# Grouped attention: three rounded products for scores and values, probabilities scaled on GpSimd, a weight split in four pieces

## The reference, cut to what matters

```python
B, SQ, HIDDEN = (2, 256, 256)
HEADS, GROUPS, KVC = (16, 4, 128)
HPG = HEADS // GROUPS
LAYER_INDEX = 1
SCALE = KVC ** (-0.5)
b, sq, _ = x.shape
...
q = jnp.einsum('bsh,he->bse', x, w_q).reshape(b, sq, GROUPS, HPG, KVC)
kv = jnp.einsum('bsh,he->bse', x, w_kv)
k, v = jnp.split(kv, 2, axis=-1)
...
scores = jnp.einsum('bqgpd,bkgd->bgqpk', q, k) * (SCALE / LAYER_INDEX)
...
causal = jnp.arange(sq)[:, None] >= jnp.arange(sk)[None, :]
scores = jnp.where(causal[None, None, :, None, :], scores, -jnp.inf)
probs = jax.nn.softmax(scores, axis=-1).astype(x.dtype)
ctx = jnp.einsum('bgqpk,bkgd->bqgpd', probs, v).reshape(b, sq, HEADS * KVC)
return jnp.einsum('bse,eh->bsh', ctx, w_dense)
```

## Time and profile before

| | |
|---|---|
| median of 3 runs (lowest to highest) | 1756.77 us (1753.88 to 1758.28) |
| profiled execution, its time | 1758.49 us |
| profiled execution, first to last instruction (span) | 1756.7 us |
| mean granted clock of TensorE | 0.955 |
| busy over the span: TensorE, VectorE, ScalarE, GpSimd | 1578.6, 1052.2, 868.1, 376.4 us |
| grouped attention (258.2 to 535.7 us): TensorE, VectorE, ScalarE, GpSimd busy | 260.78, 143.35, 136.96, 16.48 us |

### The profile page before, as it was taken

How to read it: one execution, slowest core, us unless ns; L and a number is a source line. 1 busy time by engine, 2 the same in 40 slices (tenths; PEclk the granted TensorE clock), 3 DMA queues, 4 the chain that set the end, 5 groups by cost and what they waited for, 6 DMA issues and landing times. The chain is left out here.

```text
span 1756.7 us, 27299 instructions
## 1 busy us (share of the span) xinstructions
PE 1578.6 (90%) x9658; PEld 1270.8 (72%) x9658; DVE 1052.2 (60%) x2079; ACT 868.1 (49%) x1931; POOL 376.4 (21%) x400
## 2 busy tenths in 40 slices
PE   7789989999999889998678869879999999997987
PEld 6568866766768768886356646658888888875966
DVE  2665445374465544445558750657878787876965
ACT  2443334454455333333357643446666666664634
POOL 0044531011002054543454212101101010001300
PEclk9789989999999899999889988899999999998999
DMA  4131111000000463220144320100000000001000
GB/s 119 48 116 49 48 33 35 6 13 18 0 0 1 128 156 99 77 79 1 26 69 62 39 74 1 44 21 16 19 9 18 9 18 18 9 1 50 1 0 25
DMA packets 76099, 68.23 MB, mean 39 GB/s; under 512 B 32176, under 2 KB 67208, under 8 KB 76016
## 3 DMA queue, kind: packets, MB, share of 16 engines
q1 hardware_dynamic: 71312, 62.73, 13.5%
q0 software_dynamic: 4704, 4.40, 2.0%
HBM read 56.46 MB, written 1.21 MB: 33 GB/s over the span
## 5 line engine op out<-in xcount | busy, mean ns | idle before, releaser
L2326 ACT ACTIVATE diff_att_probs<-psum,diff_att_neg_max 128x512 f32<-128x512 f32 x256 | 174.4, 695 | 27.3 <-DVE diff_att_neg_max L2388 27.3
L2388 DVE TENSOR_REDUCE diff_att_neg_max<-psum 128x2 f32<-128x1024 f32 x128 | 153.1, 1218 | 24.1 <-PE psum L2226 24.1
L2247 PE MATMUL psum<-diff_att_v_tok,diff_att_mixed_t 128*128 128x128 f32 x1024 | 127.5, 279 | 0.8 <-ACT diff_att_mixed_t L2332 0.8
L2247 PEld LDWEIGHTS psum<-diff_att_v_tok,diff_att_mixed_t 128*128 128x128 f32 x1024 | 124.3, 196 | 4.5 <-issue 1.8
L1346 ACT ACTIVATE gqa_att_probs<-psum,gqa_att_neg_max 128x128 f32<-128x128 f32 (+3 forms) x128 | 66.4, 524 | 69.0 <-DVE gqa_att_neg_max L1378 69.0
L472 POOL TENSOR_TENSOR ahead_w_hi<-ahead_w,ahead_zeros 128x512 fp32r<-128x512 f32 x16 | 16.6, 1039 | 375.2 <-DMA ahead_w<-in_L_attn_Wv 375.1
L1378 DVE TENSOR_REDUCE gqa_att_neg_max<-psum 128x1 f32<-128x128 f32 (+3 forms) x128 | 53.8, 483 | 70.0 <-PE psum L1296 69.0
L892 POOL TENSOR_TENSOR top_scaled<-top_scaled,top_wb 128x512 f32<-128x512 f32 x48 | 65.3, 1366 | 117.1 <-DVE top_scaled L871 87.1
L2400 DVE SCALAR_TENSOR_TENSOR diff_att_mixed<-diff_att_probs,diff_att_ratio 128x512 f32<-128x512 f32 x128 | 87.7, 748 | 1.1
L871 DVE TENSOR_TENSOR top_scaled<-top_gate,psum 128x512 f32<-128x512 f32 x48 | 32.9, 687 | 86.5 <-PE psum L101 64.6
L1640 POOL DMA_DIRECT2D mla_att_q_own<-mla_att_parts x144 | 71.0, 502 | 54.5 <-PE psum L1726 50.5
(11 more groups left out here) (480 smaller groups left out, 4586.3 us busy)
## 6 DMA issues: line engine op xcount, KB each, us to landing
top_wb<-top_w_dram SPq DMA_DIRECT2D x16, 384.0 KB, 4.1
golden_wb<-golden_w_dram SPq DMA_DIRECT2D x8, 512.0 KB, 4.8
top_wb<-top_w_dram SPq DMA_DIRECT2D x16, 256.0 KB, 4.3
mla_att_k_feat<-mla_att_parts SPq DMA_DIRECT2D x56, 64.0 KB, 4.5
mla_att_q_own<-mla_att_parts POOLq DMA_DIRECT2D x112, 32.0 KB, 3.5
top_w_nat<-in_L_ffn_w SPq DMA_DIRECT2D x16, 192.0 KB, 3.1
top_w_nat<-in_L_ffn_v SPq DMA_DIRECT2D x16, 192.0 KB, 4.2
top_down_w<-in_L_ffn_w SPq DMA_DIRECT2D x1, 3072.0 KB, 13.2
```

The lines of the kernel that those rows point to most:

```text
L2247: last = nc.tensor.matmul(bank[6][:, qt * P:(qt + 1) * P], mixed_t[:, u % 2, kt, qt * P:(qt + 1) * P], v_tok[:, slot, b * QT + kt, :], sta ...
L2326: last = nc.scalar.activation(probs[:, qt, m, :], bank[2 * (qt % 2) + m], ACT.Exp, bias=neg_max[:, qt, m:m + 1], accum_out=row_sum[:, qt, ...
L2388: nc.vector.tensor_reduce(neg_max[:, qt, :], psum[:, 2 * (qt % 2):2 * (qt % 2) + 2, :], AX.X, ALU.max, negate=True).then_inc(maxed, 1)
```

## The change

The scores and the values become three rounded products each. For that every projection is rounded to a high part by ScalarE (now q_hi, k_hi, v_hi) and VectorE subtracts it from the bank to get the low part (`lower_projection`); a bank is free for the next job when the low part is made. The turned probabilities are treated in the same way: ScalarE copies banks 4 and 5 to `pt_hi`, VectorE bank 7, and VectorE makes the three low parts (`lower_turned`). `attend` waits bank by bank. The scaling of the probabilities moves from VectorE to GpSimd, as a multiplication by a reciprocal that is spread over the row. The split of the next group's weights is cut in its four instructions, which stand on GpSimd ahead of the scaling of units 2 to 5. The probabilities are packed without gaps.

```diff
+
+    def split_part(self, pool, g, i):
+
+        nc, t, rounded = self.nc, self.t, self.sem["w_rounded"]
+        n = "kq"[i % 2]
+        raw, high, low = (t[f"w{n}_{part}"] for part in ("g", "hi", "lo"))
+        if i == 0:
+            pool.wait_ge(self.sem["w_loaded"], g * 48 + 48)
+        if i < 2:
+            nc.gpsimd.tensor_tensor(high[:], raw[:], t["zeros"][:].to_broadcast([P, DC, raw.shape[2]]), ALU.add).then_inc(rounded, 1)
+        else:
+            pool.wait_ge(rounded, g * 2 + (i - 1))
+            nc.gpsimd.tensor_tensor(low[:], raw[:], high[:].bitcast(F32), ALU.subtract).then_inc(self.sem["w_split"], 1)
 
...
-            q_feat = at.sb("q_feat", [P, HPG, T])
-            k_feat = at.sb("k_feat", [P, T])
-            v_tok = at.sb("v_tok", [P, NT, HD])
-            probs = at.sb("probs", [P, 2, QT, SEQ])
-            probs_t = at.sb("probs_t", [P, QT, SEQ])
+            q_hi, q_lo = (at.sb(f"q_{n}", [P, HPG, T], F32R) for n in ("hi", "lo"))
+            k_hi, k_lo = (at.sb(f"k_{n}", [P, T], F32R) for n in ("hi", "lo"))
...
+            probs = at.sb("probs", [P, 2, PACKED])
+            pt_hi, pt_lo = (at.sb(f"pt_{n}", [P, PACKED], F32R) for n in ("hi", "lo"))
+            row = lambda s, qt: probs[:, s, qt * (qt + 1) // 2 * P:(qt + 1) * (qt + 2) // 2 * P]
+            turned = [slice(0, 4 * P), slice(4 * P, 7 * P), slice(7 * P, 10 * P)]
+            turned_bank = [bank[4], bank[5][:, 0:3 * P], bank[7][:, 0:3 * P]]
...
-                with pool.Fori(1, GROUPS) as g:
-                    pool.wait_ge(proj_made, g * JOBS)
-                    pre.split(pool, g)
+                def normalise(g, u):
+                    s = u % 2
+                    pool.wait_ge(inverted, g * UNITS + (u + 1))
+                    for qt in range(QT):
+                        tile = row(s, qt)
+                        last = nc.gpsimd.tensor_tensor(tile, tile, inv_sum[:, s, qt:qt + 1].to_broadcast([P, (qt + 1) * P]), ALU.mult)
+                    last.then_inc(probs_ready, 1)
+
+                with pool.Fori(0, GROUPS - 1) as g:
+                    for u in range(UNITS):
+                        if 2 <= u < 6:
+                            pre.split_part(pool, g + 1, u - 2)
+                        normalise(g, u)
+                for u in range(UNITS):
+                    normalise(GROUPS - 1, u)
...
-                        pe.wait_ge(proj_read, g * JOBS + (j - 2))
+                        pe.wait_ge(proj_low, g * JOBS + (j - 2))
...
-                        nc.tensor.matmul(bank[qt][:, 0:(qt + 1) * P], q_feat[:, h, b * SEQ + qt * P:b * SEQ + (qt + 1) * P],
-                                         k_feat[:, b * SEQ:b * SEQ + (qt + 1) * P], start=True, stop=False)
+                        queries = slice(b * SEQ + qt * P, b * SEQ + (qt + 1) * P)
+                        keys = slice(b * SEQ, b * SEQ + (qt + 1) * P)
+                        product3(nc, bank[qt][:, 0:(qt + 1) * P], (q_hi[:, h, queries], q_lo[:, h, queries]),
+                                 (k_hi[:, keys], k_lo[:, keys]), start=True, stop=False)
...
-                    pe.wait_ge(t_read_act, g * UNITS + (u + 1))
-                    pe.wait_ge(t_read_dve, g * (2 * UNITS) + 2 * (u + 1))
                     if u:
                         pe.wait_ge(ctx_read, g * UNITS + u)
+                    at = 0
                     for kt in range(QT):
-                        last = nc.tensor.matmul(bank[6][:, kt * P:SEQ], v_tok[:, b * QT + kt, :],
-                                                probs_t[:, kt, 0:SEQ - kt * P], start=kt == 0, stop=kt == QT - 1)
+                        if kt < 3:
+                            pe.wait_ge(t_low, g * (3 * UNITS) + (3 * u + kt + 1))
+                        part = slice(at, at + SEQ - kt * P)
+                        at += SEQ - kt * P
+                        last = product3(nc, bank[6][:, kt * P:SEQ], (v_hi[:, b * QT + kt, :], v_lo[:, b * QT + kt, :]),
+                                        (pt_hi[:, part], pt_lo[:, part]), start=kt == 0, stop=kt == QT - 1)
...
-                        causal_transposes(nc, env, lambda qt: probs[:, u % 2, qt, :], t_made)
+                        causal_transposes(nc, env, lambda qt: row(u % 2, qt), t_made)
...
+                        read = nc.scalar.activation(q_hi[:, h, cols], job_bank(j), ACT.Copy, scale=SCALE)
                     elif kind == "k":
...
-                        act.wait_ge(t_made, g * (3 * UNITS) + (3 * u + 1))
-                        nc.scalar.activation(probs_t[:, 0, :], bank[4][:], ACT.Copy).then_inc(t_read_act, 1)
+                        for k in range(2):
+                            act.wait_ge(t_made, g * (3 * UNITS) + (3 * u + k + 1))
+                            nc.scalar.activation(pt_hi[:, turned[k]], turned_bank[k], ACT.Copy).then_inc(t_high_act, 1)
...
-                    dve.wait_ge(inverted, g * UNITS + (u + 1))
-                    for qt in range(QT):
-                        tile = probs[:, s, qt, 0:(qt + 1) * P]
-                        last = nc.vector.tensor_scalar(tile, tile, inv_sum[:, s, qt:qt + 1], None, ALU.mult)
-                    last.then_inc(probs_ready, 1)
...
+                def lower_projection(g, j):
+                    kind, h, half = jobs[j]
+                    cols, tiles = slice(half * HALF, (half + 1) * HALF), slice(4 * half, 4 * half + 4)
+                    dve.wait_ge(proj_high, g * JOBS + (j + 1))
+                    if kind == "q":
+                        low = nc.vector.scalar_tensor_tensor(q_lo[:, h, cols], job_bank(j), SCALE, q_hi[:, h, cols].bitcast(F32),
+                                                             ALU.mult, ALU.subtract)
+                    elif kind == "k":
+                        low = nc.vector.tensor_tensor(k_lo[:, cols], job_bank(j), k_hi[:, cols].bitcast(F32), ALU.subtract)
...
+                    low.then_inc(proj_low, 1)
...
+                def lower_turned(g, u, k):
+                    if k < 2:
+                        dve.wait_ge(t_high_act, g * (2 * UNITS) + (2 * u + k + 1))
+                    else:
+                        dve.wait_ge(t_high_dve, g * UNITS + (u + 1))
+                    nc.vector.tensor_tensor(pt_lo[:, turned[k]], turned_bank[k], pt_hi[:, turned[k]].bitcast(F32),
+                                            ALU.subtract).then_inc(t_low, 1)
...
                 with dve.Fori(0, GROUPS) as g:
-                    maxima(g, 0)
-                    normalise(g, 0)
+                    for j in range(JOBS):
+                        lower_projection(g, j)
+                        if j == EARLY:
+                            maxima(g, 0)
+                        if j == JOBS - 2:
+                            normalise(g, 0)
                     for u in range(UNITS):
                         if u + 1 < UNITS:
                             maxima(g, u + 1)
-                        dve.wait_ge(t_made, g * (3 * UNITS) + (3 * u + 2))
-                        nc.vector.tensor_copy(probs_t[:, 1, 0:3 * P], bank[5][:, 0:3 * P]).then_inc(t_read_dve, 1)
+                        lower_turned(g, u, 0)
                         dve.wait_ge(t_made, g * (3 * UNITS) + (3 * u + 3))
-                        nc.vector.tensor_copy(probs_t[:, 2, 0:2 * P], bank[7][:, 0:2 * P])
-                        nc.vector.tensor_copy(probs_t[:, 3, 0:P], bank[7][:, 2 * P:3 * P]).then_inc(t_read_dve, 1)
+                        nc.vector.tensor_copy(pt_hi[:, turned[2]], turned_bank[2]).then_inc(t_high_dve, 1)
+                        lower_turned(g, u, 1)
+                        lower_turned(g, u, 2)
                         if u + 1 < UNITS:
                             normalise(g, u + 1)
```

More of the change, by code:

```diff
@@ L1335, in read_projection @@
                     if kind == "q":
[L1336 removed]
+                        read = nc.scalar.activation(q_hi[:, h, cols], job_bank(j), ACT.Copy, scale=SCALE)
                     elif kind == "k":
[L1338 removed]
+                        read = nc.scalar.activation(k_hi[:, cols], job_bank(j), ACT.Copy)
                     else:
[L1340 to L1341 removed]
+                        read = nc.scalar.activation(v_hi[:, 4 * half:4 * half + 4, :].rearrange("p t e -> p (t e)"), job_bank(j), ACT.Copy)
+                    read.then_inc(proj_high, 1)
                 def exps(g, u, *qts):
@@ L1345, in exps @@
                         act.wait_ge(maxed, g * (UNITS * QT) + (u * QT + qt + 1))
-                        nc.scalar.activation(probs[:, u % 2, qt, 0:(qt + 1) * P], bank[qt][:, 0:(qt + 1) * P], ACT.Exp,
+                        nc.scalar.activation(row(u % 2, qt), bank[qt][:, 0:(qt + 1) * P], ACT.Exp,
                                              bias=neg_max[:, u % 2, qt:qt + 1],
@@ L1384, in normalise @@
                     nc.vector.reciprocal(inv_sum[:, s, :], row_sum[:, s, :]).then_inc(inverted, 1)
-                    dve.wait_ge(inverted, g * UNITS + (u + 1))
-                    for qt in range(QT):
-                        tile = probs[:, s, qt, 0:(qt + 1) * P]
```

(20 more changed lines are left out.)

14 lines of the change are left out of this document (6 added, 8 removed).

## The result

The changed kernel takes 1791.62 us (median of 4 runs, 1783.66 to 1792.96) against 1756.75 of the kernel before (1753.88 to 1758.28, 4 runs): a ratio of 1.017, 95% interval 1.0143 to 1.0197, so it is slower, by 35 us. The forecast was 1781, range 1769 to 1800.

A forecast was written before the change was run, and what follows sets the result against it. TensorE bounds attention now; afterwards a 6.45 us loop through ScalarE, VectorE and GpSimd would. 25.7 - 0.6 + 0.7, less 1 for the clock, gave +25 on 1758.49, against the runs' median 1781.8, stated as 1781 us; range 1769 to 1800.

The forecast's parts named there:

- The loop: Grouped attention: transposes, ScalarE copy, VectorE subtractions, reciprocal, GpSimd scaling, next transposes take 6.45 us per interval, against 5.69 now.
- The cheaper products are worth nothing: Scores and values: TensorE's work per unit falls 0.6 us to 5.06, but lies wholly in the shadow of 6.45 us.
- First intervals: First unit of a group: ScalarE's exponentials come first, delaying the copy of bank 4 by 1.79 us: 8.24 us.
- Last intervals: Last unit of a group, without scores beside it: ended early by TensorE before, afterwards as long as the others.
- The split: Next group's weight split on GpSimd: four pieces of 0.6 to 2.4 us fit in 3.6 us idle and cost nothing.
- TensorE's clock: Granted clock after TensorE's waits: as many falls as now, one, at 1.6 us; less 1 us in the sum.
- End and start of a group: Last transposes to next projection 4.15 us instead of 4.29, less 0.6 over four groups; wait for last projection +0.7.
- the rate of two full operands: GpSimd's scaling takes 3.4 us, 0.5 to 0.6 more per interval, +15: 1796 us; chance 0.12.
- rival 2: TensorE's clock falls again and again, 1.6 us each, in one interval of three of 28, +15: 1796 us; chance 0.09.
- the rival for a gain: GpSimd is not late and TensorE stays the bound: intervals of 5.06 to 5.1 us, 1743 us; chance 0.07.
- the price of 1.9 us: GpSimd's four multiplications must be done in 1.9 us, 1.5 ns per column with nothing per instruction, for a gain.
- the row of chances: List of outcome chances: the forecast itself, a loop of 6.1 to 6.8 us, had 0.68 for 1771 to 1791 us.

The follow-up runs named there:

- early reciprocal: Changed kernel with the reciprocal of unit u+1 moved right behind its row maxima, ahead of unit u's copy and three subtractions: 1740.95 us, ratio to before 0.9892.
- filler in the gaps: Changed kernel with unused bf16 products on TensorE, 8 ahead of and 4 behind each group's last transposes: 1784.65 us, ratio to before 1.0144.

## Why the prediction was right, and where it was off

**The loop was right link by link.** From the start of the transposes: copy after 0.69 us (forecast 0.64), subtraction after 1.32 (1.32), reciprocal after 3.33 (3.33), GpSimd after 3.57 (3.58), the next transposes 2.81 after that (2.88). Together 6.38 against 6.45. TensorE's idle time, forecast at 1.4 us, is the interval less its work, 6.38 - 5.19 = 1.19, of which the profile shows 1.00 as idle. The hand-over to TensorE was rather 0.05 than 0.08 us, and GpSimd 2.76 rather than 2.8. The early reciprocal shows that the order is the cause, the tile left unscaled that GpSimd's time counts whole.

**"The cheaper products are worth nothing" was right.** Without two thirds of them the interval is the same wherever the clock held, and never shorter. Their own price was slightly off: with the early reciprocal TensorE bounds the unit and 5.19 us is its work, 5.06 forecast; a 128-column product costs 0.12 us there (0.37 for three, from 310.78 to 311.15) where I took 0.10.

**First intervals** are 8.10 to 8.11 us, forecast 8.24. **Last intervals** are as long as the others, 6.38, as forecast. The 28 intervals gave +22.7 instead of +25.7. Of the 3.0 us, 24 x 0.07 + 4 x 0.13 = 2.2 are shorter intervals, less 0.8 for a fall of the clock behind the first unit in two groups (6.79 and 6.84 us); the other 1.6 are the fall that the kernel before had behind a first unit, which the forecast took apart, as 1. A second fall of the kernel before, in its first projections, the forecast did not see; it stands behind the ledger's -1.3.

**The split was right**, free in four pieces and 1.8 us a group in one.

**The step that was mis-sized is TensorE's clock.** "I take as many falls as now, one" gave -1, and "End and start of a group" +0.1; behind the last transposes of the four groups the profile shows +7.3 and +3.4, 10.7 us. The step did not see that the last unit has no scores: TensorE's work in it is only transposes and values, so a loop of 6.38 us leaves 0.98 and 1.93 us of idle time, one behind the other, instead of 1.0. The clock fell there in all four groups, 9.9 us in all, and with filler in the gaps it did not. Against the sum of 24.8 us the stage gave 32.1: 10.6 more by this term, 2.0 less by the intervals (with the -1) and 1.3 less by the first projections. Two misses in the other direction made the total look closer than the term was. What is left, 0.8 us (28.03 instead of 27.82 three times and 7.67 instead of 7.47), is the end and start of a group proper, forecast at 0.1.

**The rivals.** GpSimd did not scale at the rate of two full operands (the rival's four terms add up to 3.46 us, not 3.4; measured 2.76), and no instruction of VectorE was stretched beside it. The clock fell again and again, as rival 2 had it, but it did not lengthen the steady intervals: the 1.0 us gaps there were followed by full-speed transposes. Behind the waits of 1.9 us in the first unit it fell in two groups of four, at 0.4 us each instead of 1.6: the profile shows no idle time before the next transposes there. That rival was half right, and its place was the end of a group, beside the forecast's loop and not instead of it. TensorE staying the bound, the rival for a gain, did not happen in this kernel; it is what the early reciprocal makes of it (1740.95, the rival's 1743), by an order of the queue and not by the price of 1.9 us that I had named as its only way.

The lower end of the range does not follow from its own figure: a loop of 6.1 us gives 1771, as the row of chances has it, and not 1769. Nothing hangs on it here.

**Left open**: why the clock fell behind some first units and not behind others. It was not tested.

## What to carry to other kernels

A split into high and low parts costs the engines that make the parts, and where an instruction that the next unit waits for stands behind them in the same queue, their whole length enters the loop; write the loop out across all engines before pricing the products, and move the small instruction (here a reciprocal of 0.17 us, worth 51 us, 10 of them through the clock) ahead of them. An engine change alone, to a slower engine, is neither good nor bad: ask what stood behind the work on the old queue. When a loop grows past TensorE's work, look at the units with the least work beside them, at the ends of the pipeline: there the idle time comes together, and here the clock fell there.

## What the runs showed of the hardware

A GpSimd multiplication in place by a reciprocal that is spread over the row took 401, 615, 829 and 1043 ns for 128 to 512 columns: 1.67 ns per column and 0.19 us per instruction, against 2.17 ns for two full operands.

VectorE's subtractions, one operand in PSUM and one in SBUF, and its rounding copies out of PSUM took 0.69 and 0.55 us beside a running GpSimd (the early reciprocal's timeline), the same as alone; its scaling inside SBUF stood still beside GpSimd before (5.20 instead of 1.27 us). The Trainium skill (SBUF — State Buffer, "Who interferes with whom") has the lock on the shared port pair taken by the scaling form, and not by an instruction with a single SBUF input outside the modes that use both port pairs. The trace agrees with both halves.

TensorE's transposes behind a gap of 1.0 us in the steady intervals took 1.31 us, full speed. In the last units, with gaps of 0.98 and 1.93 us and only transposes and values between, the granted clock fell in all four groups (0.57 to 0.76 in the windows shown). Behind waits of 1.9 us in first units it fell in two of four groups, and with three of four tiles scaled, where the gaps in the last units were 0.98 and 0.95 us, in one of four.
